# Window attention recurrence: the new score from an unnormalised sum, a maximum over the older scores, and each row held twice

## The chip, the cores and the metric

The kernel runs on one core of a Trainium2 chip. Its time is the device time of one execution, in microseconds (us). Three runs of the kernel before gave 2842.83, 2843.85 and 2847.93 us, a median of 2843.85 us. Engines: PE is TensorE, PEld its weight loads, DVE VectorE, ACT ScalarE, POOL GpSimd, SP the engine that issues most DMAs.

## The reference

The first layer is a recurrence over 1024 tokens in 4 sequences, with a window of 64. Only this layer is touched by the change. The rest of the program (a layer norm between, then a transformer layer with attention and a mixture of experts) takes the second half of the time.

```
q_local = feature @ wq_w + wq_b
def step(buf, q_i):                      # buf: the last 64 outputs
    ki = concat([buf, zeros((B, 1, D))], axis=1)          # 65 rows, the last is zero
    scores = einsum('bwd,d->bw', q_i[:, None, :] * ki, w2_w) + w2_b[0]
    alpha = softmax(scores, axis=1)
    v_i = einsum('bwd,bw->bd', ki, alpha)
    return concat([buf[:, 1:, :], v_i[:, None, :]], axis=1), v_i
_, vs = scan(step, feature[:, :64, :], q_local[:, 64:, :])
```

Each output is a weighted sum of the 64 outputs ahead of it, so token after token must be computed in turn: 960 steps.

## The kernel before

**Chunks and rows.** The 960 steps are 30 chunks (`NC`) of 32 rows (`L`). The kernel never forms an output inside the chunk's loop. It keeps, in `tab`, three tables of 96 columns: table 0 holds scores and tables 1 and 2 hold coefficients by which a row depends on the 64 outputs ahead of the chunk. The 128 partitions are 4 sequences of 32: for the scores, a partition is a future query of the chunk; for the coefficients, it is one of the older outputs. Since a row's output is linear in older outputs, its score against every later query is the same weighted sum of older scores. After a chunk, PE turns coefficients into outputs and computes the next chunk's first scores; that is work of a few us, mostly beside the loop.

**A step.** For row r of chunk c, with `k = r % 2`:

- ACT (L204) computes `ex = exp(row - max)` over 65 columns and its sum `z`. That is one instruction and a read of its accumulator.
- DVE then computes `rz = 1/z` (L292), the weighted sum of table 0 (helper `weighted`, L264, table 0), the *next* row's new score (L298: the sum of `ex * rz * row`, written straight into column 64 of `row`), the weighted sum of table 1 (L264), the next row's maximum (L306), the new score of table 0 times `rz` (helper `normalised`, L269, one column), the weighted sum of table 2 (L264), a shuffle that copies row r+2 of table 0 to all partitions of its sequence (L314), and the coefficients times `rz` (L269, two columns).

The order on DVE is written by hand; every engine takes its instructions in that order. `s_exp`, `s_rz`, `s_new`, `s_max`, `s_raw_score`, `s_score`, `s_row`, `s_raw` and `s_coef` are semaphores between them. Of two waits ahead of an operation, the first is an instruction of its own, and `sem_inc(s_pace, 1)` behind a `wait_ge` makes such a lone instruction too. `s_pace` itself is waited for by nobody.

**Row buffers.** `row` has two buffers of 66 columns: the next row's scores stand in columns 1 to 65, and columns 0 to 64 are the same scores as the row before it sees them, one place to the left.

Of the kernel before, what the change touches and what calls it, by code (L numbers as in the profile page):

```python
# [10 lines left out]
ALU = mybir.AluOpType  # L11
ACT = mybir.ActivationFunctionType
AX = mybir.AxisListType

P = 128
B, T, D = 4, 1024, 128
WIN = 64
L = 32
NK = T // L
NC = NK - WIN // L  # L20
ROW = WIN + 1
# [17 lines left out]
M_ROW = HD * PARTS  # L39
EPS = 1e-5  # L40


def window_attention(nc, io, xt, w, stacks, s_weights, moe_dram):

# [2 lines left out]
    with ctx:  # L47
        def sb(name, shape, dt=F32):
            return ctx.enter_context(nc.sbuf_tensor(name, shape, dt))
# [4 lines left out]
        def sem(name):  # L54
            return ctx.enter_context(nc.semaphore(name))
# [23 lines left out]


        tab = sb("tab", [P, 3, WIN + L])
        row = sb("row", [P, 2, ROW + 1])
        nmax = sb("nmax", [P, 2])
        ex = sb("ex", [P, 2, ROW])
        z = sb("z", [P, 2])
        rz = sb("rz", [P, 2])
        junk = sb("junk", [P, 4, ROW])
        raw = sb("raw", [P, 3])

        pf = ps("pf", [P, 2, 4 * P])  # L90
        pq = ps("pq", [P, 2, 4 * P])
# [11 lines left out]
        s_pace, s_pace_act = sem("s_pace"), sem("s_pace_act")  # L103
# [4 lines left out]
        s_scores = sem("s_scores")  # L108
        s_row, s_max, s_exp, s_rz, s_new, s_coef = (sem("s_row"), sem("s_max"), sem("s_exp"), sem("s_rz"),
                                                   sem("s_new"), sem("s_coef"))  # L110
        s_raw, s_raw_score, s_score = sem("s_raw"), sem("s_raw_score"), sem("s_score")
        s_clear = sem("s_clear")
        s_bdc, s_pv, s_vr, s_vall, s_pt, s_vt2, s_vt1, s_g, s_bdg = (
            sem("s_bdc"), sem("s_pv"), sem("s_vr"), sem("s_vall"), sem("s_pt"), sem("s_vt2"), sem("s_vt1"),
# [72 lines left out]
        @block.scalar  # L187
        def _(act):
            act.wait_ge(s_mv, NK)
            act.wait_ge(s_const, 2)  # L190
            nc.scalar.activation(std[:, :], mv[:, :, 1], ACT.Sqrt, bias=eps[:, :]).then_inc(s_std, 1)
            for g in range(8):
                act.wait_ge(s_ft, g + 1)
                if g >= 2:
                    act.wait_ge(s_pq, g - 1)
                if g == 2:
                    act.wait_ge(s_vt0, 2)
                nc.scalar.copy(ft[:, g % 2, :], pf[:, g % 2, :]).then_inc(s_ftc, 1)
            nc.scalar.preload_act_table(ACT.Exp)
            act.wait_ge(s_init, 14)  # L200
            for c in range(NC):
                for r in range(L):
                    act.wait_ge(s_max, L * c + r + 1)
                    nc.scalar.activation(ex[:, r % 2, :], row[:, r % 2, 1:], ACT.Exp, bias=nmax[:, r % 2:r % 2 + 1],  # L204
                                         accum_out=z[:, r % 2:r % 2 + 1]).then_inc(s_exp, 1)


                    if r == 1:
                        act.wait_ge(s_vall, c + 1)
                        act.sem_inc(s_pace_act, 1)  # L210
                        act.wait_ge(s_pv, c + 1)
                        nc.scalar.copy(vr[:, :], p_v[:, 0:D]).then_inc(s_vr, 1)
                    if r == 4:
                        act.wait_ge(s_vt2, c + 1)
                        act.sem_inc(s_pace_act, 1)
                        act.wait_ge(s_pt, c + 1)
                        nc.scalar.copy(vt1[:, :], p_t[:, 0:P]).then_inc(s_vt1, 1)
                    if 8 <= r < 8 + B:
                        act.wait_ge(s_g, c + 1)
                        q = slice(L * (r - 8), L * (r - 8) + L)  # L220
                        nc.scalar.copy(bdg[q, :, q], p_g[q, 0:2 * P].rearrange("p (g i) -> p g i", g=2)[:, :, q])\  # L221
                            .then_inc(s_bdg, 1)

        @block.vector
        def _(dve):
# [29 lines left out]
            for b in range(B):  # L255
                q = slice(L * b, L * b + L)
# [4 lines left out]

            def weighted(g, k, r, done):

                nc.vector.scalar_tensor_tensor(junk[:, g, :], ex[:, k, :], 1.0, tab[:, g, r:r + ROW], ALU.mult,  # L264
                                               ALU.mult, accum_out=raw[:, g:g + 1]).then_inc(done, 1)

            def normalised(g0, g1, k, r, done):

                nc.vector.tensor_tensor(tab[:, g0:g1, r + WIN:r + ROW], raw[:, g0:g1].unsqueeze(2),  # L269
                                        rz[:, k:k + 1].unsqueeze(1).broadcast_to((P, g1 - g0, 1)),  # L270
                                        ALU.mult).then_inc(done, 1)

            for c in range(NC):
                nc.vector.tensor_copy(tab[:, 0, WIN:], b0_row[:, :]).then_inc(s_table, 1)
                dve.wait_ge(s_scores, c + 1)
                nc.vector.tensor_scalar(tab[:, 0, 0:WIN], p_s[:, 0:WIN], b0[:, :], None, ALU.add).then_inc(s_table, 1)
                dve.wait_ge(s_table, 2 * (c + 1))
                dve.sem_inc(s_pace, 1)

                nc.vector.stream_shuffle(row[:, 0, 1:], tab[:, 0, 0:ROW], [0] * L).then_inc(s_row, 1)  # L280
                nc.vector.stream_shuffle(row[:, 1, :], tab[:, 0, 0:ROW + 1], [1] * L).then_inc(s_row, 1)
                dve.wait_ge(s_row, L * c + 1)
                nc.vector.reduce_max(nmax[:, 0:1], row[:, 0, 1:], AX.X, negate=True).then_inc(s_max, 1)

                dve.wait_ge(s_bdc, c + 1)
                nc.vector.memset(tab[:, 1:3, WIN:], 0.0).then_inc(s_clear, 1)
                dve.wait_ge(s_clear, c + 1)
                for r in range(L):
                    k, n = r % 2, L * c + r
                    last = r == L - 1  # L290
                    dve.wait_ge(s_exp, n + 1)
                    nc.vector.reciprocal(rz[:, k:k + 1], z[:, k:k + 1]).then_inc(s_rz, 1)  # L292
                    if not last:
                        weighted(0, k, r, s_raw_score)

                        dve.wait_ge(s_row, L * c + r + 2)
                        dve.wait_ge(s_rz, n + 1)
                        nc.vector.scalar_tensor_tensor(junk[:, 3, :], ex[:, k, :], rz[:, k:k + 1],  # L298
                                                       row[:, 1 - k, 0:ROW], ALU.mult, ALU.mult,
                                                       accum_out=row[:, 1 - k, WIN:ROW]).then_inc(s_new, 1)  # L300
                    if r:
                        dve.wait_ge(s_coef, n)
                    weighted(1, k, r, s_raw)
                    if not last:
                        dve.wait_ge(s_new, (L - 1) * c + r + 1)
                        nc.vector.reduce_max(nmax[:, 1 - k:2 - k], row[:, 1 - k, 1:], AX.X, negate=True)\  # L306
                            .then_inc(s_max, 1)
                        dve.wait_ge(s_raw_score, (L - 1) * c + r + 1)
                        normalised(0, 1, k, r, s_score)
                    weighted(2, k, r, s_raw)  # L310
                    if r < L - 2:
                        dve.wait_ge(s_score, (L - 1) * c + r + 1)
                        dve.sem_inc(s_pace, 1)
                        nc.vector.stream_shuffle(row[:, k, :], tab[:, 0, r + 1:r + 2 + ROW], [r + 2] * L)\  # L314
                            .then_inc(s_row, 1)
                    dve.wait_ge(s_raw, 2 * n + 2)
                    normalised(1, 3, k, r, s_coef)

            dve.wait_ge(s_pv, NC + 1)
            nc.vector.tensor_copy(v_all[:, NC + 2, :], p_v[:, 0:D]).then_inc(s_vr, 1)  # L320
# [1422 lines left out]
```

## Time and profile before

| | |
|---|---|
| median of 3 runs | 2843.85 us |
| profiled execution | 2847.15 us |
| span of its trace | 2845.3 us |
| DVE busy | 2248.1 us, 79% |
| ACT busy | 1286.1 us, 45% |
| PE busy | 1189.3 us, 42% |

The profiled execution is 3.3 us above the median. The busy time is the time covered by an engine's instructions. On DVE consecutive instructions overlap: the next begins before the one ahead of it has ended, so the distance from start to start is what an instruction takes of the engine, and the duration is what a waiting instruction has to wait for. Both are read from the timeline. A DVE or ACT instruction with an accumulator is two rows, the operation and the read of its accumulator; only at the end of the second is the sum there. Lone waits are not among the timeline's rows.

### The profile page before, as it was taken

To read this page: it belongs to the slowest core of one execution; us is meant where nothing else is said; L and a number is where in the kernel's file an instruction comes from. 1 tells how busy PE (TensorE), PEld (TensorE's weight loads), DVE (VectorE), ACT (ScalarE), POOL (GpSimd) and SP (SyncE) were. 2 spreads that over 40 slices of the span, in tenths; PEclk is the share of its full clock that TensorE was granted. 3 is DMA by queue.
4 is the path that set the end of the run, shared out by engine and by line. 5 is a ranking of instruction groups with operands and counts; after the bars stand their busy time and mean duration, and the time that the engine had idled before them with its cause. 6 is when DMAs were issued, how large, how long until landed. Compare 5 with 4: busy or idle time off the path is not lost. (4 is left out here: it accounts for less than half of the span.)

```text
span 2845.3 us, 38133 instructions
## 1 busy us (share of the span) xinstructions
PE 1189.3 (42%) x7272; PEld 529.5 (19%) x7272; DVE 2248.1 (79%) x15205; ACT 1286.1 (45%) x3230; POOL 287.0 (10%) x425
## 2 busy tenths in 40 slices
PE   3010100001010101000003787878877877787797
PEld 1000000000000000000001111223422333233365
DVE  5999999999999999999994789776767667765233
ACT  1333333333333333333361456557855676577742
POOL 0000000000000000000010020032113210321211
PEclk9999999999999999999997799889988898799998
DMA  5000000000000000000015012103110211100100
GB/s 136 1 1 1 1 1 1 1 1 1 1 1 1 1 1 1 1 1 1 1 32 133 8 31 56 20 21 82 38 44 21 65 46 30 33 23 27 41 1 23
DMA packets 80181, 66.13 MB, mean 23 GB/s; under 512 B 8702, under 2 KB 64808, under 8 KB 79944
## 3 DMA queue, kind: packets, MB, share of 16 engines
q1 hardware_dynamic: 76872, 57.40, 8.3%
q0 software_dynamic: 3072, 6.30, 0.7%
q14 instruction: 177, 1.45, 0.2%
q8 instruction: 60, 0.98, 0.1%
HBM read 34.77 MB, written 28.57 MB: 22 GB/s over the span
## 5 line engine op out<-in xcount | busy, mean ns | idle before, releaser
L1310 DVE TENSOR_REDUCE nm_half<-pair 128x2 f32<-128x1024 f32 x512 | 611.6, 1220 | 196.7 <-PE pair L1558 178.4
L204 ACT ACTIVATE ex<-row,nmax 128x65 f32<-128x65 f32 x960 | 336.1, 350 | 924.2 <-DVE nmax L306 837.6
L1198 ACT ACTIVATE pt<-pair 128x1024 f32<-128x1024 f32 x512 | 513.6, 1025 | 382.7 <-PE pair L1568 368.1
L264 DVE SCALAR_TENSOR_TENSOR junk<-ex,tab 128x65 f32<-128x65 f32 x2850 | 622.1, 219 | 1.4 <-issue 0.4
L367 PE MATMUL p_s<-tab,bdg 128*128 128x32 f32 x120 | 31.9, 406 | 829.4 <-DVE tab L269 829.4
L1534 PE MATMUL p_o<-pt,va 128*9 128x512 f32 x2048 | 298.4, 658 | 7.0 <-ACT pt L1198 7.0
L269 DVE TENSOR_TENSOR tab<-raw,rz 128x1 f32<-128x1 f32 (+1 forms) x1890 | 286.6, 152 | 3.2 <-issue 1.1
L298 DVE SCALAR_TENSOR_TENSOR junk<-ex,rz,row 128x65 f32<-128x65 f32 x930 | 265.5, 285 | 3.0 <-issue 2.7
L1558 PE MATMUL pair<-ks,qs 48*128 48x512 bf16 x1024 | 209.5, 420 | 111.7 <-ACT pt L1198 55.8
L264 DVE DVE_READ_ACCUMULATOR junk<-ex,tab 128x1 f32 x2850 | 236.8, 83 | 0.2
L1568 PE MATMUL pair<-qs,ks 50*128 50x512 bf16 x1024 | 210.8, 415 | 52.6 <-ACT pt L1198 22.1
L314 DVE STREAM_SHUFFLE row<-tab 128x66 f32<-128x66 f32 x900 | 207.0, 230 | 10.2 <-issue 2.6
L306 DVE TENSOR_REDUCE nmax<-row 128x1 f32<-128x65 f32 x930 | 200.6, 216 | 0.4
L367 PEld LDWEIGHTS p_s<-tab,bdg 128*128 128x128 f32 x120 | 27.9, 323 | 833.4 <-DVE tab L269 833.4
L204 ACT ACTIVATION_READ_ACCUMULATOR ex<-row,nmax 128x1 f32 x960 | 179.2, 187 | 0.0
L292 DVE RECIPROCAL rz<-z 128x1 f32<-128x1 f32 x960 | 157.1, 164 | 18.6 <-ACT ex L204 15.1
L182 POOL TENSOR_TENSOR bdc<-tab,mask 128x128 f32<-128x128 f32 x60 | 26.0, 455 | 1226.3 <-DVE tab L269 1226.3
L364 PE MATMUL p_s<-vt,qn 128*32 128x32 f32 x240 | 10.0, 251 | 255.2 <-ACT bdg L221 255.2
L1568 PEld LDWEIGHTS pair<-qs,ks 50*128 50x128 bf16 x1024 | 48.6, 95 | 304.9 <-DVE nm_half L1310 122.1
L1222 ACT ACTIVATE hid<-pair,bias_t 128x128 f32<-128x128 f32 x276 | 75.3, 383 | 28.6 <-PE pair L1633 28.4
L1558 PEld LDWEIGHTS pair<-ks,qs 48*128 48x128 bf16 x1024 | 49.5, 97 | 202.3 <-ACT pt L1198 91.8
L1633 PE MATMUL pair<-hid,yg 128*128 128x128 f32 x552 | 75.2, 292 | 25.5 <-DVE nm_half L1310 16.0
(254 smaller groups left out, 1951.1 us busy)
## 6 DMA issues: line engine op xcount, KB each, us to landing
parts_dram<-parts SPq DMA_DIRECT2D x48, 256.0 KB, 3.5
qs<-parts_dram SPq DMA_DIRECT2D x32, 192.0 KB, 4.7
ks<-parts_dram SPq DMA_DIRECT2D x32, 192.0 KB, 5.2
hid<-xs_dram SPq DMA_DIRECT2D x33, 128.0 KB, 2.1
ys_dram<-hid SPq DMA_DIRECT2D x33, 128.0 KB, 1.8
h_dram<-f SPq DMA_DIRECT2D x20, 128.0 KB, 2.5
x<-in_x SPq DMA_DIRECT2D x4, 512.0 KB, 8.3
w_W<-in_W SPq DMA_DIRECT2D x1, 2048.0 KB
```

Of the source, the lines that this page charges most:

```text
L204: nc.scalar.activation(ex[:, r % 2, :], row[:, r % 2, 1:], ACT.Exp, bias=nmax[:, r % 2:r % 2 + 1], accum_out=z[:, r % 2:r % 2 + 1]).then_i ...
L264: nc.vector.scalar_tensor_tensor(junk[:, g, :], ex[:, k, :], 1.0, tab[:, g, r:r + ROW], ALU.mult, ALU.mult, accum_out=raw[:, g:g + 1]).the ...
L269: nc.vector.tensor_tensor(tab[:, g0:g1, r + WIN:r + ROW], raw[:, g0:g1].unsqueeze(2), rz[:, k:k + 1].unsqueeze(1).broadcast_to((P, g1 - g0 ...
L292: nc.vector.reciprocal(rz[:, k:k + 1], z[:, k:k + 1]).then_inc(s_rz, 1)
L298: nc.vector.scalar_tensor_tensor(junk[:, 3, :], ex[:, k, :], rz[:, k:k + 1], row[:, 1 - k, 0:ROW], ALU.mult, ALU.mult, accum_out=row[:, 1 ...
L306: nc.vector.reduce_max(nmax[:, 1 - k:2 - k], row[:, 1 - k, 1:], AX.X, negate=True)\
L314: nc.vector.stream_shuffle(row[:, k, :], tab[:, 0, r + 1:r + 2 + ROW], [r + 2] * L)\
L1198: nc.scalar.activation(pt[:, kt % 2, :, tokens(t)], pair[fill.pair][:, :, :], ACT.Exp, scale=SCALE).then_inc(s_exp, 1)
L1310: nc.vector.reduce_max(nm_half[:, t, hp % 2, :, q], pair[fill.pair][:, :, :], AX.X, negate=True)\
L1534: ins = nc.tensor.matmul(p_o[j:j + VH, :], va[:, kt, 2 * (hp % HP) + par, :], pt[:, kt % 2, par, tokens(t)], start=kt == 0, stop=kt == QT - 1)
L1558: ins = nc.tensor.matmul(pair[fill.pair][:, par, :], qs[rows, hp % HP, tile(q)], ks[rows, hp % HP, tokens(t)], start=True, stop=True)
L1568: ins = nc.tensor.matmul(pair[fill.pair][:, par, :], ks[rows, hp, tile(kt)], qs[rows, hp, tokens(t)], start=True, stop=True)
```

## The change

It does the following, in the first layer alone:

- `weighted` holds the exponentials to `CAP` = 1e30 by a minimum instead of multiplying them by 1.
- The next row's new score is computed in two instructions: a weighted sum with unnormalised exponentials into `raw[:, 3]` (L313 of the new kernel), which stands ahead of the reciprocal, and a small operation on one column, `max(rz, 1/CAP) * raw` (helper `divided`, L274), which writes it into the row.
- `normalised` becomes `divided`, the same small operation as a `scalar_tensor_tensor`.
- The maximum (`largest`, L290) is over `row[:, :, 0, 1:]`, 64 columns without the new score, and stands ahead of the small operation that writes the new score. ACT waits for both the maximum and the new score.
- Each row buffer holds two copies, one as the row before sees it, the other shifted by one. One shuffle (`shifted`, L286) of 130 columns writes both, in place of one of 66.
- The order in a step is: sum for the new score, reciprocal, sum of table 0, maximum, new score, score into table 0, coefficients of the *row before*, shuffle, sums of tables 1 and 2.

```diff
+CAP = 1e30
...
-        row = sb("row", [P, 2, ROW + 1])
+        row = sb("row", [P, 2, 2, ROW])
...
-        raw = sb("raw", [P, 3])
+        raw = sb("raw", [P, 4])
...
                     act.wait_ge(s_max, L * c + r + 1)
-                    nc.scalar.activation(ex[:, r % 2, :], row[:, r % 2, 1:], ACT.Exp, bias=nmax[:, r % 2:r % 2 + 1],
+                    if r:
+                        act.sem_inc(s_pace_act, 1)
+                        act.wait_ge(s_new, (L - 1) * c + r)
+                    nc.scalar.activation(ex[:, r % 2, :], row[:, r % 2, 1, :], ACT.Exp, bias=nmax[:, r % 2:r % 2 + 1],
                                          accum_out=z[:, r % 2:r % 2 + 1]).then_inc(s_exp, 1)
...
-                nc.vector.scalar_tensor_tensor(junk[:, g, :], ex[:, k, :], 1.0, tab[:, g, r:r + ROW], ALU.mult,
+                nc.vector.scalar_tensor_tensor(junk[:, g, :], ex[:, k, :], CAP, tab[:, g, r:r + ROW], ALU.min,
                                                ALU.mult, accum_out=raw[:, g:g + 1]).then_inc(done, 1)
...
+            def divided(to, g0, g1, k, done):
+                nc.vector.scalar_tensor_tensor(to, rz[:, k:k + 1].unsqueeze(1).broadcast_to((P, g1 - g0, 1)),
+                                               1.0 / CAP, raw[:, g0:g1].unsqueeze(2), ALU.max, ALU.mult)\
+                    .then_inc(done, 1)
+            def coefficients(c, r):
+                dve.wait_ge(s_raw, 2 * (L * c + r) + 2)
+                divided(tab[:, 1:3, r + WIN:r + ROW], 1, 3, r % 2, s_coef)
+            def shifted(q, r):
+                src = tab[:, 0, r:r + ROW]
+                pair = bass.AP(src.tensor, src.offset, [src.ap[0], [1, 2], [1, ROW]])
+                nc.vector.stream_shuffle(row[:, q % 2, :, :], pair, [q] * L).then_inc(s_row, 1)
+            def largest(c, r):
+                dve.wait_ge(s_row, L * c + r + 1)
+                nc.vector.reduce_max(nmax[:, r % 2:r % 2 + 1], row[:, r % 2, 0, 1:], AX.X, negate=True)\
+                    .then_inc(s_max, 1)
...
                     dve.wait_ge(s_exp, n + 1)
+                    if not last:
+                        dve.wait_ge(s_row, n + 2)
+                        nc.vector.scalar_tensor_tensor(junk[:, 3, :], ex[:, k, :], CAP, row[:, 1 - k, 0, :], ALU.min,
+                                                       ALU.mult, accum_out=raw[:, 3:4]).then_inc(s_raw_new, 1)
                     nc.vector.reciprocal(rz[:, k:k + 1], z[:, k:k + 1]).then_inc(s_rz, 1)
                     if not last:
                         weighted(0, k, r, s_raw_score)
-
-                        dve.wait_ge(s_row, L * c + r + 2)
+                    if not last:
+                        largest(c, r + 1)
+                    if not last:
+                        dve.wait_ge(s_raw_new, m)
+                        dve.sem_inc(s_pace, 1)
                         dve.wait_ge(s_rz, n + 1)
-                        nc.vector.scalar_tensor_tensor(junk[:, 3, :], ex[:, k, :], rz[:, k:k + 1],
-                                                       row[:, 1 - k, 0:ROW], ALU.mult, ALU.mult,
-                                                       accum_out=row[:, 1 - k, WIN:ROW]).then_inc(s_new, 1)
+                        divided(row[:, 1 - k, 1, WIN - 1:WIN].unsqueeze(2), 3, 4, k, s_new)
+                    if not last:
+                        dve.wait_ge(s_raw_score, m)
+                        divided(tab[:, 0:1, r + WIN:r + ROW], 0, 1, k, s_score)
+                    if r:
+                        coefficients(c, r - 1)
+                    if r < L - 2:
+                        dve.wait_ge(s_score, m)
+                        dve.sem_inc(s_pace, 1)
+                        shifted(r + 2, r + 1)
                     if r:
                         dve.wait_ge(s_coef, n)
                     weighted(1, k, r, s_raw)
-                    if not last:
-                        dve.wait_ge(s_new, (L - 1) * c + r + 1)
-                        nc.vector.reduce_max(nmax[:, 1 - k:2 - k], row[:, 1 - k, 1:], AX.X, negate=True)\
-                            .then_inc(s_max, 1)
-                        dve.wait_ge(s_raw_score, (L - 1) * c + r + 1)
-                        normalised(0, 1, k, r, s_score)
                     weighted(2, k, r, s_raw)
-                    if r < L - 2:
-                        dve.wait_ge(s_score, (L - 1) * c + r + 1)
-                        dve.sem_inc(s_pace, 1)
-                        nc.vector.stream_shuffle(row[:, k, :], tab[:, 0, r + 1:r + 2 + ROW], [r + 2] * L)\
-                            .then_inc(s_row, 1)
-                    dve.wait_ge(s_raw, 2 * n + 2)
-                    normalised(1, 3, k, r, s_coef)
+                    if last:
+                        coefficients(c, r)
```

The order on DVE, one step inside a chunk of the kernel before, from its reciprocal to the next (L264 is `weighted` for tables 0, 1 and 2 in turn, L269 `normalised`):

```order
L292 RECIPROCAL rz<-z 128x1 [waits s_exp]
L264 SCALAR_TENSOR_TENSOR junk,raw<-ex,tab 128x65
L298 SCALAR_TENSOR_TENSOR junk,row<-ex,rz,row 128x65 [waits s_rz,s_row]
L264 SCALAR_TENSOR_TENSOR junk,raw<-ex,tab 128x65 [waits s_coef]
L306 TENSOR_REDUCE nmax<-row 128x1 [waits s_new]
L269 TENSOR_TENSOR tab<-raw,rz 128x1 [waits s_raw_score]
L264 SCALAR_TENSOR_TENSOR junk,raw<-ex,tab 128x65
L314 STREAM_SHUFFLE row<-tab 128x66 [waits s_score]
L269 TENSOR_TENSOR tab<-raw,rz 128x2 [waits s_raw]
L292 RECIPROCAL rz<-z 128x1 [waits s_exp]
```

The same stretch of the changed kernel, from the first instruction that waits for ACT to the next such (L269 is now `weighted`, L274 `divided`, L286 the shuffle, L290 the maximum):

```order
L313 SCALAR_TENSOR_TENSOR junk,raw<-ex,row 128x65 [waits s_row,s_exp]
L315 RECIPROCAL rz<-z 128x1
L269 SCALAR_TENSOR_TENSOR junk,raw<-ex,tab 128x65
L290 TENSOR_REDUCE nmax<-row 128x1 [waits s_row]
L274 SCALAR_TENSOR_TENSOR row<-rz,raw 128x1 [waits s_raw_new,s_rz]
L274 SCALAR_TENSOR_TENSOR tab<-rz,raw 128x1 [waits s_raw_score]
L274 SCALAR_TENSOR_TENSOR tab<-rz,raw 128x2 [waits s_raw]
L286 STREAM_SHUFFLE row<-tab 128x130 [waits s_score]
L269 SCALAR_TENSOR_TENSOR junk,raw<-ex,tab 128x65 [waits s_coef]
L269 SCALAR_TENSOR_TENSOR junk,raw<-ex,tab 128x65
L313 SCALAR_TENSOR_TENSOR junk,raw<-ex,row 128x65 [waits s_row,s_exp]
```

Nine instructions have become ten. The shuffle has moved ahead of the sums of tables 1 and 2, and between it and the score that it waits for (the one-column L274 that writes `tab`) there is now a two-column operation instead of a sum over 65 columns.

The last two rows of a chunk on DVE, in the changed kernel (from the sum of table 1 in row 30 to the copy that opens the next chunk's table):

```order
L269 SCALAR_TENSOR_TENSOR junk,raw<-ex,tab 128x65 [waits s_coef]
L269 SCALAR_TENSOR_TENSOR junk,raw<-ex,tab 128x65
L315 RECIPROCAL rz<-z 128x1 [waits s_exp]
L274 SCALAR_TENSOR_TENSOR tab<-rz,raw 128x2 [waits s_raw]
L269 SCALAR_TENSOR_TENSOR junk,raw<-ex,tab 128x65 [waits s_coef]
L269 SCALAR_TENSOR_TENSOR junk,raw<-ex,tab 128x65
L274 SCALAR_TENSOR_TENSOR tab<-rz,raw 128x2 [waits s_raw]
L294 COPY tab<-b_row 128x32
```

Here the coefficients of row 30 stand between the reciprocal of row 31 and its sums; before, they stood ahead of that reciprocal.

## Rows read from the trace of the kernel before

**Rows 1.** The page's busy times: engine, us, share of the span, instructions.

```profile
PE 1189.3 (42%) x7272; PEld 529.5 (19%) x7272; DVE 2248.1 (79%) x15205; ACT 1286.1 (45%) x3230; POOL 287.0 (10%) x425
```

**Rows 2.** Busy time by stretch, first layer's loop: stretch, length, each engine, clock, DMA.

```profile
56.90:1440.00 1383.10, 126.68 (x633) 95.61 (x634) 1297.33 (x13380) 457.43 (x2100) 49.09 (x150) 1.00 0.00 1
```

**Rows 3.** Waits of DVE, 58 to 1440 us: who, for whom: us, times, longest.

```profile
DVE rz L292 <- ACT ex L204: 15.1, 30, 0.6
DVE row L314 <- issue: 5.5, 15, 0.4
```

**Rows 4.** The same for ACT.

```profile
ACT ex L204 <- DVE nmax L306: 837.6, 930, 1.3
```

**Rows 5.** Timeline of one step: start us, duration us, engine, line, operation.

```profile
690.83 0.16 DVE L292 RECIPROCAL rz<-z 128x1 f32<-128x1 f32 x1
690.91 0.21 DVE L264 SCALAR_TENSOR_TENSOR junk<-ex,tab 128x65 f32<-128x65 f32 x1
691.04 0.08 DVE L264 DVE_READ_ACCUMULATOR junk<-ex,tab 128x1 f32 x1
691.11 0.28 DVE L298 SCALAR_TENSOR_TENSOR junk<-ex,rz,row 128x65 f32<-128x65 f32 x1
691.32 0.08 DVE L298 DVE_READ_ACCUMULATOR junk<-ex,rz,row 128x1 f32 x1
691.32 0.22 DVE L264 SCALAR_TENSOR_TENSOR junk<-ex,tab 128x65 f32<-128x65 f32 x1
691.46 0.09 DVE L264 DVE_READ_ACCUMULATOR junk<-ex,tab 128x1 f32 x1
691.46 0.22 DVE L306 TENSOR_REDUCE nmax<-row 128x1 f32<-128x65 f32 x1
691.60 0.15 DVE L269 TENSOR_TENSOR tab<-raw,rz 128x1 f32<-128x1 f32 x1
691.66 0.22 DVE L264 SCALAR_TENSOR_TENSOR junk<-ex,tab 128x65 f32<-128x65 f32 x1
691.71 0.35 ACT L204 ACTIVATE ex<-row,nmax 128x65 f32<-128x65 f32 x1 [0.92 <-DVE nmax L306]
691.80 0.09 DVE L264 DVE_READ_ACCUMULATOR junk<-ex,tab 128x1 f32 x1
691.90 0.01 DVE L314 LOAD_MASK_SELECT row<-tab  x1
691.92 0.23 DVE L314 STREAM_SHUFFLE row<-tab 128x66 f32<-128x66 f32 x1
691.97 0.19 ACT L204 ACTIVATION_READ_ACCUMULATOR ex<-row,nmax 128x1 f32 x1
692.06 0.15 DVE L269 TENSOR_TENSOR tab<-raw,rz 128x2 f32<-128x2 f32 x1
692.19 0.16 DVE L292 RECIPROCAL rz<-z 128x1 f32<-128x1 f32 x1
```

**Rows 6.** Timeline of DVE where a chunk begins.

```profile
702.41 0.28 DVE L276 TENSOR_SCALAR tab<-p_s,b 128x64 f32<-128x64 f32 x1 [1.07 <-PE p_s L367]
702.85 0.01 DVE L280 LOAD_MASK_SELECT row<-tab  x1 [0.15 <-DVE tab L276]
702.88 0.23 DVE L280 STREAM_SHUFFLE row<-tab 128x65 f32<-128x65 f32 x1
...
703.94 0.16 DVE L292 RECIPROCAL rz<-z 128x1 f32<-128x1 f32 x1 [0.50 <-ACT ex L204]
```

**Rows 7.** Timeline of DVE around row 30 of that chunk, and the next chunk.

```profile
745.17 0.15 DVE L269 TENSOR_TENSOR tab<-raw,rz 128x2 f32<-128x2 f32 x1
745.45 0.16 DVE L292 RECIPROCAL rz<-z 128x1 f32<-128x1 f32 x1
...
746.81 0.16 DVE L292 RECIPROCAL rz<-z 128x1 f32<-128x1 f32 x1
...
748.61 0.28 DVE L276 TENSOR_SCALAR tab<-p_s,b 128x64 f32<-128x64 f32 x1 [1.06 <-PE p_s L367]
```

More of the change, by code:

```diff
@@ L110, in window_attention @@
                                                    sem("s_new"), sem("s_coef"))
-        s_raw, s_raw_score, s_score = sem("s_raw"), sem("s_raw_score"), sem("s_score")
+        s_raw, s_raw_score, s_score, s_raw_new = sem("s_raw"), sem("s_raw_score"), sem("s_score"), sem("s_raw_new")
         s_clear = sem("s_clear")
@@ L262, in weighted @@
             def weighted(g, k, r, done):
-                nc.vector.scalar_tensor_tensor(junk[:, g, :], ex[:, k, :], 1.0, tab[:, g, r:r + ROW], ALU.mult,
+                nc.vector.scalar_tensor_tensor(junk[:, g, :], ex[:, k, :], CAP, tab[:, g, r:r + ROW], ALU.min,
                                                ALU.mult, accum_out=raw[:, g:g + 1]).then_inc(done, 1)
[L267 to L271, printed above, removed]
+            def divided(to, g0, g1, k, done):
[13 more added lines that the diff above has]
+                    .then_inc(s_max, 1)
             for c in range(NC):
@@ L278, in _ @@
                 dve.sem_inc(s_pace, 1)
-                nc.vector.stream_shuffle(row[:, 0, 1:], tab[:, 0, 0:ROW], [0] * L).then_inc(s_row, 1)
-                nc.vector.stream_shuffle(row[:, 1, :], tab[:, 0, 0:ROW + 1], [1] * L).then_inc(s_row, 1)
+                nc.vector.stream_shuffle(row[:, 0, 1, :], tab[:, 0, 0:ROW], [0] * L).then_inc(s_row, 1)
+                shifted(1, 0)
                 dve.wait_ge(s_row, L * c + 1)
-                nc.vector.reduce_max(nmax[:, 0:1], row[:, 0, 1:], AX.X, negate=True).then_inc(s_max, 1)
+                nc.vector.reduce_max(nmax[:, 0:1], row[:, 0, 1, :], AX.X, negate=True).then_inc(s_max, 1)
                 dve.wait_ge(s_bdc, c + 1)
@@ L288, in _ @@
                 for r in range(L):
-                    k, n = r % 2, L * c + r
+                    k, n, m = r % 2, L * c + r, (L - 1) * c + r + 1
                     last = r == L - 1
                     dve.wait_ge(s_exp, n + 1)
+                    if not last:
+                        dve.wait_ge(s_row, n + 2)
+                        nc.vector.scalar_tensor_tensor(junk[:, 3, :], ex[:, k, :], CAP, row[:, 1 - k, 0, :], ALU.min,
+                                                       ALU.mult, accum_out=raw[:, 3:4]).then_inc(s_raw_new, 1)
                     nc.vector.reciprocal(rz[:, k:k + 1], z[:, k:k + 1]).then_inc(s_rz, 1)
```

## The prediction

> **What bounds the kernel now.** I began with the page's busy times: DVE has 79% of the span, ACT 45% [rows 1]. Then the stretches: the first layer's loop takes 1383 of 2845 us, DVE is busy in 1297 of them, ACT in 457, and PE and POOL hardly at all [rows 2]. So everything that the change touches is one engine with hardly a gap, and one beside it that mostly waits. The waits say for what: ACT waits 837.6 us for the maximum of L306, once in each of 930 steps, while DVE waits for ACT only 30 times, once a chunk [rows 3, 4]. That looks like a loop bound by DVE alone, but the timeline of a step says something finer. From reciprocal to reciprocal a step takes 692.19 - 690.83 = 1.36 us. The reciprocal at 692.19 begins 0.03 after ACT's accumulator read has ended (691.97 + 0.19 = 692.16), and 0.13 after the two-column L269, though behind the one-column L269 the next instruction began after 0.06 [rows 5]. So ACT releases it, and DVE has about 0.06 us to spare in a step. Two things are nearly equal: the ring (reciprocal, L264, L298, L264, maximum, ACT, reciprocal), 1.36 us, and the time that DVE needs for its instructions, 1.30 us.
>
> **The ring after the change.** I put 0 at the start of the new sum L313 and go by starts in [rows 5], each good to 0.01. What an instruction takes of DVE: a sum with an immediate 0.145 (0.14 from 691.32 to 691.46, where the next begins together with the accumulator read; 0.15 can be the rounding), 0.13 for the one behind the reciprocal (690.91 to 691.04), the reciprocal 0.08, the maximum 0.135, a small operation 0.065. Reciprocal at 0.145, table 0 at 0.225, maximum at 0.355, new score at 0.49, done at 0.64 (0.15 long). ACT starts 0.03 behind its releaser (691.46 + 0.22 = 691.68, start 691.71), at 0.67; if the maximum (end 0.575) and the lone wait in front set it, hardly later. It needs 0.45 (691.71 to 692.16), so it has done at 1.12, and the next sum could start at about 1.16, or 1.22 with the lone wait of `s_exp` in front. So the change does what it says: the ring falls from 1.36 to 1.16 to 1.22. Gone from it are L298's longer stay (0.21 for 0.145, with the 0.07 ahead of it) and the sum of table 1.
>
> **What DVE needs.** New score at 0.49, score into table 0 at 0.555, ending at 0.705, coefficients at 0.62. Now comes the shuffle, which waits for that score, with a lone wait and then the mask load ahead of it. What this costs stands in the trace, since the same pair was there: L269 ended at 691.60 + 0.15 = 691.75, the mask load came at 691.90 and the shuffle at 691.92, 0.17 later; where a chunk begins and nothing else is in the way it is 702.69 to 702.88, 0.19 [rows 5, 6]. Before, the sum of table 2 (0.14) ran in that time; now only the two-column operation (0.065) does. So the shuffle starts at 0.705 + 0.175 = 0.88, and DVE issues nothing from 0.685 to 0.86. That stall of 0.17 is the heart of my forecast.
>
> The shuffle has 130 columns instead of 66. No row shows that size. Below, it takes of DVE what 66 columns do, 0.14 (691.92 to 692.06); above, two such, 0.28. Between them: 65 columns against 1 cost 0.145 against 0.065 for the two-tensor operations, 0.08 for 64 columns, so I take 0.14 + 0.07 = 0.21. Then come the two sums at 1.09 and 1.235, and the next L313 at 1.38. ACT has done at 1.12, long before.
>
> So the step is 1.38 us against 1.36: DVE now sets it. Ten roundings can put this off by about 0.02. The sums have 0.14 and 0.15 beside each other, and the place of the shuffle 0.17 and 0.19; leaning to the larger I take 1.385, 0.025 more than before. The ring's gain of 0.14 or more is lost behind DVE: saved there are 0.06 at L298 and 0.07 ahead of it, and paid are one instruction more (0.065), 0.07 of columns and about 0.08 of stall that a sum used to cover; against a step of 1.30 on DVE that is 0.08 more. `min` in place of `mult`, the maximum over 64 columns and `max` in the small operation change neither count nor columns: nothing. The third and further lone waits (in front of L313 for ACT, in front of the new score) are for events that came at least 0.1 us earlier, and I cost them at nothing because the sequencer meets them while the instruction ahead runs; if that cover is missing, each costs about what a lone wait adds between a satisfied release and its operation, 0.05 to 0.07 (L298 began 0.07 behind the accumulator read's start, where L306 began at once).
>
> **Chunk edges.** A chunk took 748.61 - 702.41 = 46.20 us [rows 6, 7]. The second shuffle at its start is longer by 0.07 and stands ahead of the first maximum: +0.07. Row 30 has no shuffle, so there the ring sets the end: about 1.16 instead of 1.38, -0.20 against before. In row 31 the coefficients of row 30 stand behind the reciprocal, and the sum of table 1 waits for them: 0.08 + 0.15 + 0.03 instead of 0.08, +0.18. Together +0.05 a chunk, 1.5 us in all. PE's and POOL's work between chunks is as before.
>
> **Fetch stalls.** 32 steps of 1.36 and the edges do not make up 46.20: now and then a step is longer, as at 745.45, where the reciprocal comes 0.28 behind L269 instead of 0.13 [rows 5, 7]; the profile names "issue" for 15 of those ahead of the shuffle alone [rows 3]. 46.20 - 1.53 (L276 at 702.41 to the first reciprocal) - 31 x 1.36 - 1.80 (the last reciprocal to L276 at 748.61) leaves 0.7 us a chunk, 21 us in all. With an instruction more in nine and nothing to spare, I estimate 3 to 6 more; I take 4.
>
> **Sum.** 900 steps with a shuffle x 0.025 = 22.5, edges 1.5, stalls 4: +28 us, within what a row rounded to 0.01 allows +30. On the profiled execution, 2847.15 + 30 = 2877; on the median, 3.3 lower, 2874 us.
>
> **Rivals.**
> - *The wait for the score is not paid; the ring sets the end (faster).* If DVE could issue mask and shuffle behind the coefficients without the 0.17, its need would be 1.38 - 0.17 = 1.21, and the ring 1.22 at most: -0.14 x 930 = -130 us, about 2714. For it: the ring does shorten, and the score's release falls in a part where DVE still has coefficients to do. Against: 0.17 and 0.19 in both places of the trace where this pair stands, once with nothing between. It decides from where the stall falls under 0.15 (no loss). Chance 0.09.
> - *Each instruction takes the least that a row shows, or the long shuffle no more than the short one.* With 0.13 for every sum and the maximum, 0.06 for a small operation and 0.20 for the shuffle the step is 1.315; with my prices and 0.14 for the shuffle it is the same. That is less than now: -0.045 x 900 + 5 = -35 us, 2809 on the median. For it: 0.13 does stand behind the reciprocal. Against: 0.14 and 0.15 stand behind the others [rows 5]. The Trainium skill (VectorE: DVE Perf Modes, the section on the TRN2 errata) has 58 cycles and one for each element, at 0.96 GHz, which is 0.128 for a sum, 0.061 for a small operation and 0.196 for this shuffle; by it the step would be 1.28 and the time about 2775. The rows are 0.01 to 0.02 above it for each sum, and with four of them, and a maximum, in a step that decides the sign. Chance 0.05.
> - *It comes out level:* the ten roundings fall the other way by 0.025 a step. 2838 to 2849. Chance 0.06.
> - *Lone waits are not covered, or the shuffle costs double.* +0.055 a step for the wait in front of L313 makes +50 on top of mine, about 2924; a shuffle of 0.28 makes +63, about 2937. For the first: behind table 0's sum the wait in front of L298 did cost 0.07. Against: that wait's own release, the reciprocal (end 690.99), came late enough to explain it. Chance 0.14.
> - *Each added DVE instruction costs a whole one.* Nine instructions take 1.36, 0.151 each; ten would take 1.51, +0.15 x 930 = +140, 2984. Against: instructions begin 0.14 apart though 0.22 long, and small ones 0.06 apart [rows 5]. The Trainium skill's rule that one should minimise the number of chained VectorE operations, since the pipe drains behind each (VectorE: DVE Perf Modes, "Rules for kernel authors"), speaks for it. Chance 0.03.
>
> My forecast has the remaining 0.63, with 2852 to 2900 as its own range. What a measurement of this kernel can tell from no change is about 0.2%, 6 us. Faster by more: 0.09 + 0.05 = 0.14. Within: 0.06. Slower, with 0.63, 0.14 and 0.03: 0.80. For 8 in 10 the range leaves out the faster cases and the highest: 2842 to 2922.
>
> **What would show it.** In the new timeline: L313 to L313 1.38 to 1.39 us; between the two-column L274 and the mask load DVE idle for about 0.17; shuffle to the next sum 0.21; ACT's accumulator read ending 0.2 or more ahead of the next L313, so that DVE waits for ACT in rows 31 and 0 alone; ACT's start set by the maximum or the new score near 0.67 to 0.73. It is wrong if the idle piece ahead of the mask load is missing, if L313 comes 0.03 to 0.1 behind ACT's end, or if L313 starts later than 0.15 behind the sum of table 2.

## The result, and the profile after

The changed kernel takes 2871.49 us (median of 4 runs, 2868.01 to 2876.24), the kernel before 2843.34 us (4 runs): a ratio of 1.0099, with a 95% interval of 1.0081 to 1.0117. That is 28 us slower, and the interval leaves out no change. The forecast was 2874 us, 30 more than the kernel before.

The page of the changed kernel, its busy times, answers to [rows 1]:

```profile
PE 1179.6 (41%) x7272; PEld 526.0 (18%) x7272; DVE 2208.3 (77%) x16135; ACT 1286.0 (45%) x3230; POOL 288.9 (10%) x425
```

DVE has 930 instructions more, one a step, and is busy 40 us *less*. That does not tell what was added: busy time is what the instructions cover with their full length, not what they take of the engine. Where DVE really stands can be read only from start to start, in a step. The timeline of the changed kernel (start us, duration us, engine, line, operation), from the new sum L313 ahead of one reciprocal to the next reciprocal, answers to [rows 5]; L274 x2 is the table's score and the coefficients:

```profile
699.22 0.22 DVE L313 SCALAR_TENSOR_TENSOR junk<-ex,row 128x65 f32<-128x65 f32 x1
699.36 0.08 DVE L313 DVE_READ_ACCUMULATOR junk<-ex,row 128x1 f32 x1
699.36 0.16 DVE L315 RECIPROCAL rz<-z 128x1 f32<-128x1 f32 x1
699.44 0.21 DVE L269 SCALAR_TENSOR_TENSOR junk<-ex,tab 128x65 f32<-128x65 f32 x1
699.57 0.08 DVE L269 DVE_READ_ACCUMULATOR junk<-ex,tab 128x1 f32 x1
699.57 0.22 DVE L290 TENSOR_REDUCE nmax<-row 128x1 f32<-128x64 f32 x1
699.70 0.15 DVE L274 SCALAR_TENSOR_TENSOR row<-rz,raw 128x1 f32<-128x1 f32 x1
699.77 0.23 DVE L274 SCALAR_TENSOR_TENSOR tab<-rz,raw 128x1 f32<-128x1 f32 x2
699.91 0.35 ACT L209 ACTIVATE ex<-row,nmax 128x65 f32<-128x65 f32 x1 [0.94 <-DVE row L274]
700.08 0.01 DVE L286 LOAD_MASK_SELECT row<-tab  x1
700.10 0.30 DVE L286 STREAM_SHUFFLE row<-tab 128x130 f32<-128x130 f32 x1
700.16 0.19 ACT L209 ACTIVATION_READ_ACCUMULATOR ex<-row,nmax 128x1 f32 x1
700.30 0.22 DVE L269 SCALAR_TENSOR_TENSOR junk<-ex,tab 128x65 f32<-128x65 f32 x1
700.45 0.08 DVE L269 DVE_READ_ACCUMULATOR junk<-ex,tab 128x1 f32 x1
700.45 0.22 DVE L269 SCALAR_TENSOR_TENSOR junk<-ex,tab 128x65 f32<-128x65 f32 x1
700.60 0.09 DVE L269 DVE_READ_ACCUMULATOR junk<-ex,tab 128x1 f32 x1
700.60 0.22 DVE L313 SCALAR_TENSOR_TENSOR junk<-ex,row 128x65 f32<-128x65 f32 x1
700.74 0.08 DVE L313 DVE_READ_ACCUMULATOR junk<-ex,row 128x1 f32 x1
700.74 0.16 DVE L315 RECIPROCAL rz<-z 128x1 f32<-128x1 f32 x1
```

The step is 1.38 us. ACT has done at 700.35, and the sum that needs it starts at 700.60, 0.25 later, behind DVE's own work: DVE sets the step. The table's score starts at 699.77 and ends at about 699.92; the shuffle starts at 700.10, and ahead of the mask load nothing is issued for about 0.17. The timeline draws half of that stretch as filled, since the two small operations together last until 700.00. Only the distance from start to start shows all of it.

Counted in this way, DVE stood in three places of a step before: 0.10 ahead of the mask load (the sum of table 2 at 691.66 takes 0.14, the mask load comes at 691.90), 0.07 ahead of L298 and 0.06 ahead of the reciprocal, 0.22 in all. Now it stands in one place, for 0.17. So DVE waits a little less than before, and its instructions take about 0.07 more of it: a small operation (0.065) and 64 columns (0.07) were added, and L298's longer stay (0.065) is gone. The new stall ahead of the shuffle uses up what the shorter waits elsewhere gave.

The same timeline at the end of a chunk and the start of the next, which answers to [rows 6, 7]:

```profile
704.87 0.16 DVE L315 RECIPROCAL rz<-z 128x1 f32<-128x1 f32 x1
...
705.89 0.16 DVE L315 RECIPROCAL rz<-z 128x1 f32<-128x1 f32 x1
705.97 0.15 DVE L274 SCALAR_TENSOR_TENSOR tab<-rz,raw 128x2 f32<-128x2 f32 x1
706.15 0.23 DVE L269 SCALAR_TENSOR_TENSOR junk<-ex,tab 128x65 f32<-128x65 f32 x1
...
707.88 0.28 DVE L296 TENSOR_SCALAR tab<-p_s,b 128x64 f32<-128x64 f32 x1 [1.07 <-PE p_s L389]
...
708.49 0.29 DVE L286 STREAM_SHUFFLE row<-tab 128x130 f32<-128x130 f32 x1
708.69 0.21 DVE L303 TENSOR_REDUCE nmax<-row 128x1 f32<-128x65 f32 x1
...
709.62 0.16 DVE L315 RECIPROCAL rz<-z 128x1 f32<-128x1 f32 x1
```

Row 30, without a shuffle, takes 1.02 us, and the last reciprocal to the next L296 1.99 in place of 1.80.

From the starts of all 960 reciprocals in the two traces, with the median of each row of a chunk as its regular length (us, first to last reciprocal):

| part | before | after | difference |
|---|---|---|---|
| rows 0 to 29 (1.360 to 1.376 in most) | 1226.0 | 1241.7 | +15.8 |
| row 30 (1.359 to 1.019) | 40.8 | 30.6 | -10.2 |
| between chunks (3.32 to 3.74) | 96.4 | 108.4 | +12.0 |
| all above the medians | 16.0 | 24.0 | +8.0 |
| sum | 1379.2 | 1404.7 | +25.6 |

The last part is the steps that are now and then 0.1 to 0.4 us longer. In the trace before, 72 of the 74 that are over 0.09 us lie a multiple of 128 recorded DVE instructions apart, lone waits and accumulator reads included. That they are pauses to fetch instructions fits, but no run tests it. The page's queue for instructions (packets, MB, share) grew by an eighth. Before:

```profile
q14 instruction: 177, 1.45, 0.2%
```

After:

```profile
q14 instruction: 199, 1.63, 0.2%
```

### The profile page after: what moved, and what is told of

Its sections match the earlier page's. It is cut to its first block and busy times, and to the rows that moved or that the text cites. A ratio compares the mean times of both kernels' runs of the same rounds, so it can differ in the third digit from the quotient of the medians.

```text
span 2868.4 us, 40893 instructions
## 1 busy us (share of the span) xinstructions
PE 1179.6 (41%) x7272; PEld 526.0 (18%) x7272; DVE 2208.3 (77%) x16135; ACT 1286.0 (45%) x3230; POOL 288.9 (10%) x425
## 5 line engine op out<-in xcount | busy, mean ns | idle before, releaser
L269 DVE SCALAR_TENSOR_TENSOR junk<-ex,tab 128x65 f32<-128x65 f32 x2850 | 545.7, 217 | 4.7
L286 DVE STREAM_SHUFFLE row<-tab 128x130 f32<-128x130 f32 x930 | 279.9, 301 | 8.2 <-issue 0.2
L269 DVE DVE_READ_ACCUMULATOR junk<-ex,tab 128x1 f32 x2850 | 236.4, 83 | 0.0
L274 DVE SCALAR_TENSOR_TENSOR tab<-rz,raw 128x1 f32<-128x1 f32 (+1 forms) x1890 | 221.4, 156 | 2.5
L313 DVE SCALAR_TENSOR_TENSOR junk<-ex,row 128x65 f32<-128x65 f32 x930 | 206.7, 222 | 15.6 <-DVE tab L305 15.3
L290 DVE TENSOR_REDUCE nmax<-row 128x1 f32<-128x64 f32 x930 | 200.6, 216 | 0.1
L274 DVE SCALAR_TENSOR_TENSOR row<-rz,raw 128x1 f32<-128x1 f32 x930 | 140.0, 151 | 2.4 <-issue 2.4
```

What stands on the lines that cost most here:

```text
L269: nc.vector.scalar_tensor_tensor(junk[:, g, :], ex[:, k, :], CAP, tab[:, g, r:r + ROW], ALU.min, ALU.mult, accum_out=raw[:, g:g + 1]).then ...
L274: nc.vector.scalar_tensor_tensor(to, rz[:, k:k + 1].unsqueeze(1).broadcast_to((P, g1 - g0, 1)), 1.0 / CAP, raw[:, g0:g1].unsqueeze(2), ALU ...
L286: nc.vector.stream_shuffle(row[:, q % 2, :, :], pair, [q] * L).then_inc(s_row, 1)
L290: nc.vector.reduce_max(nmax[:, r % 2:r % 2 + 1], row[:, r % 2, 0, 1:], AX.X, negate=True)\
L313: nc.vector.scalar_tensor_tensor(junk[:, 3, :], ex[:, k, :], CAP, row[:, 1 - k, 0, :], ALU.min, ALU.mult, accum_out=raw[:, 3:4]).then_inc( ...
```

## The experiments

My theory: DVE sets the step; the time from the end of the table's score to the shuffle, 0.177 us, is paid because only one small operation stands in it; and 64 more columns in the shuffle are paid as well. The rivals: the count of instructions decides, or the ring through ACT still does. Steps below are medians of rows 2 to 28. For comparison, the kernel before ran beside these on the same chips, at 2840.79 us (7 runs) beside "The score of table 0 first", "A lone wait less", "One copy of each row" and "A sum in the gap", and at 2842.81 us (15 runs) beside the other four.

**The score of table 0 first.** Two small operations change places, on top of the kernel called "A lone wait less" below, which the text of this expectation calls "the one before":

```diff
                     if not last:
-                        dve.wait_ge(s_raw_new, m)
-                        divided(row[:, 1 - k, 1, WIN - 1:WIN].unsqueeze(2), 3, 4, k, s_new)
-                    if not last:
                         dve.wait_ge(s_raw_score, m)
                         divided(tab[:, 0:1, r + WIN:r + ROW], 0, 1, k, s_score)
+                    if not last:
+                        dve.wait_ge(s_raw_new, m)
+                        divided(row[:, 1 - k, 1, WIN - 1:WIN].unsqueeze(2), 3, 4, k, s_new)
```

> As the one before, and the score of table 0 stands ahead of the new score of the next row, not behind it: the same instructions, two of them exchanged. Theory (the stall ahead of the shuffle counts from the end of the table's score): the score ends 0.065 earlier, so does the shuffle; step 1.31, time about 2812 us (2803 to 2822). Rival (count of instructions): step 1.375, 2871 us. Rival (ring through ACT): the next row's new score is 0.065 later, step 1.44, 2930 us.

Measured: 2798.26 us (2790.59 to 2803.84), ratio to before 0.9848 (0.9818 to 0.9879); step 1.305. The same operations, 0.07 us less a step. That the count or the ring sets the step is excluded: by the count it would have stayed, by the ring it would have risen. From this kernel's timeline:

```profile
741.68 0.15 DVE L274 SCALAR_TENSOR_TENSOR tab<-rz,raw 128x1 f32<-128x1 f32 x1
741.74 0.15 DVE L274 SCALAR_TENSOR_TENSOR row<-rz,raw 128x1 f32<-128x1 f32 x1
741.81 0.15 DVE L274 SCALAR_TENSOR_TENSOR tab<-rz,raw 128x2 f32<-128x2 f32 x1
741.98 0.01 DVE L286 LOAD_MASK_SELECT row<-tab  x1
742.00 0.30 DVE L286 STREAM_SHUFFLE row<-tab 128x130 f32<-128x130 f32 x1
```

The score ends at 741.83, and the mask load follows 0.15 and the shuffle 0.17 behind it, as in both other kernels; now two small operations run in that time.

**A lone wait less.** This changes the waits alone; the kernel above must be read against it:

```diff
             def largest(c, r):
-                dve.wait_ge(s_row, L * c + r + 1)
...
+                        dve.wait_ge(s_rz, n + 1)
                         largest(c, r + 1)
...
                         dve.wait_ge(s_raw_new, m)
-                        dve.sem_inc(s_pace, 1)
-                        dve.wait_ge(s_rz, n + 1)
                         divided(row[:, 1 - k, 1, WIN - 1:WIN].unsqueeze(2), 3, 4, k, s_new)
```

> The changed kernel without the lone wait and increment in front of the new score: the maximum waits for the reciprocal instead (its wait for the row was double), and the new score waits for its sum alone. Theory (a lone wait whose event has come runs while the instruction ahead runs, and costs nothing): step stays 1.375 us within 0.005, time 2871 within 8 us. Rival (each lone wait costs 0.05 to 0.07): step 1.31 to 1.325, time 2811 to 2825 us.

Measured, one run: 2860.02 us; step 1.375, unchanged, as expected. The time is 11 us below the changed kernel, outside the 8 that I had given. In its trace what lies above the medians inside the chunks is 17.0 us in place of 23.4, and the instruction queue has 192 packets in place of 199. So a lone wait whose event has come costs a regular step nothing. That it adds to the longer steps is likely but not shown: in the four traces with 17081 recorded DVE instructions in the loop these came to 19.9 to 26.6 us, in the three with one lone wait a step less to 17.0 to 18.3 us. That is one trace for each kernel, and the first four scatter by as much as is to be explained. The shorter time also takes a share of the credit from the exchange above: against 2860 us the exchange alone is worth 62 us, and the theory said 59.

**The coefficients moved out of the gap.** The line for the coefficients stands directly behind the reciprocal:

```diff
                     nc.vector.reciprocal(rz[:, k:k + 1], z[:, k:k + 1]).then_inc(s_rz, 1)
+                    if r:
+                        coefficients(c, r - 1)
...
-                    if r:
-                        coefficients(c, r - 1)
```

> The changed kernel with the coefficients of the row before directly behind the reciprocal, in place of between the table's score and the shuffle: the same instructions, one of them moved. Theory (the stall ahead of the shuffle counts from the end of the table's score, and the coefficients ran inside it for nothing): the score comes 0.066 later, the step 1.44, the time about 2929 us (2918 to 2940). Rival (count of instructions): 1.375, 2871 us.

Measured, one run: 2939.94 us, step 1.447, 0.072 more for the same instructions. Inside the gap that operation was free; outside it costs its place, and so the number of instructions that DVE must take outside a stall does count.

**One copy of each row.** The undoing of one part of the change (the lines that only follow the buffer's new shape are left out, here and in the next two kernels that change it):

```diff
-        row = sb("row", [P, 2, 2, ROW])
+        row = sb("row", [P, 2, ROW + 1])
...
-                nc.vector.stream_shuffle(row[:, q % 2, :, :], pair, [q] * L).then_inc(s_row, 1)
+                nc.vector.stream_shuffle(row[:, q % 2, :], tab[:, 0, r:r + ROW + 1], [q] * L).then_inc(s_row, 1)
...
-                nc.vector.reduce_max(nmax[:, r % 2:r % 2 + 1], row[:, r % 2, 0, 1:], AX.X, negate=True)\
+                nc.vector.reduce_max(nmax[:, r % 2:r % 2 + 1], row[:, r % 2, 1:WIN], AX.X, negate=True)\
```

> The changed kernel with one copy of each row (66 columns as before the change, in place of 130); the maximum is over the 63 older scores ahead of the own column, so that the new score can be written beside it. Theory (the shuffle takes one element a cycle, and its 64 columns more are paid in full on DVE): step 1.375 - 0.067 = 1.308 us, 2 us less at the chunk starts too, time about 2809 us (2800 to 2818). Rival (they are hidden behind something else that sets the step): 1.375, 2871 us.

Measured: 2804.35 us (2802.16 to 2808.17), ratio 0.9874 (0.9851 to 0.9898); step 1.308. The 64 columns cost 0.068 us a step. That is 61 us in 900 steps; the loops of the two profiles differ by 60 us, the medians by 67 us. Without these columns the change would have been a gain of 36 us.

**The doubled row in the kernel before.** The same cost, put where the ring sets the step:

```diff
-                        nc.vector.stream_shuffle(row[:, k, :], tab[:, 0, r + 1:r + 2 + ROW], [r + 2] * L)\
+                        nc.vector.stream_shuffle(row[:, k, :, :], tab[:, 0, r + 1:r + 2 + ROW].unsqueeze(1)
+                                                 .broadcast_to((P, 2, ROW + 1)), [r + 2] * L)\
```

> The kernel before, with its shuffle of 66 columns writing two copies (132 columns), of which the second is read by nobody: the doubled row alone. Theory (the kernel before is bound by the ring through ACT, with 0.06 us to spare on DVE): 0.069 more on DVE takes the spare time and makes the step 1.36 to 1.37, time 2841 to 2852 us. Rival (DVE sets the step before as well): step 1.43, 2903 us.

Measured: 2846.77 us against 2842.81, ratio 1.0009 (0.9996 to 1.0022); step 1.363. 66 more columns, 0.003 us a step: the kernel before had the 0.06 us to spare on DVE. From its timeline, where the two-column L269 is now followed by the reciprocal after 0.07, as a small operation is when nothing holds up the next one, in place of the 0.13 of [rows 5]:

```profile
741.29 0.30 DVE L314 STREAM_SHUFFLE row<-tab 128x132 f32<-128x132 f32 x1
741.50 0.15 DVE L269 TENSOR_TENSOR tab<-raw,rz 128x2 f32<-128x2 f32 x1
741.57 0.15 DVE L292 RECIPROCAL rz<-z 128x1 f32<-128x1 f32 x1
```

**A sum in the gap: a miss.** In the changed kernel, the coefficients of the row before go ahead of the maximum, and the sum of table 1 between the table's score and the shuffle:

```diff
                         weighted(0, k, r, s_raw_score)
+                    if r:
+                        coefficients(c, r - 1)
...
-                    if r:
-                        coefficients(c, r - 1)
+                    if r:
+                        dve.wait_ge(s_coef, n)
+                    weighted(1, k, r, s_raw)
                     if r < L - 2:
                         dve.wait_ge(s_score, m)
                         dve.sem_inc(s_pace, 1)
                         shifted(r + 2, r + 1)
-                    if r:
-                        dve.wait_ge(s_coef, n)
-                    weighted(1, k, r, s_raw)
```

> Same instructions as the changed kernel, in another order: the coefficients of the row before stand ahead of the maximum, and the sum of table 1 stands between the new score of table 0 and the shuffle. Theory (DVE sets the step, and the 0.17 us from the end of the table's score to the shuffle is paid because nothing fills it): the sum of table 1 fills 0.145 of it, the score itself comes 0.065 later, so the step falls from 1.375 to about 1.30 and the time from 2871 to about 2803 us (2790 to 2815), under the kernel before. Rival (each DVE instruction costs its share, whatever the order): step 1.375, 2871 us. Rival (the ring through ACT sets the step): the new score comes 0.065 later, so 2930 us.

Measured: 2861.11 us (2860.51 to 2868.15), ratio 1.0077 (1.0051 to 1.0103); step 1.370. None of the three numbers I had written down, and by the time alone the count rival looked right. The timeline says otherwise:

```profile
701.14 0.01 DVE L286 LOAD_MASK_SELECT row<-tab  x1
701.16 0.30 DVE L286 STREAM_SHUFFLE row<-tab 128x130 f32<-128x130 f32 x1
701.37 0.22 DVE L269 SCALAR_TENSOR_TENSOR junk<-ex,tab 128x65 f32<-128x65 f32 x1
701.51 0.08 DVE L269 DVE_READ_ACCUMULATOR junk<-ex,tab 128x1 f32 x1
701.58 0.23 DVE L313 SCALAR_TENSOR_TENSOR junk<-ex,row 128x65 f32<-128x65 f32 x1
```

The sum of table 1 is in the gap, but L313 now starts 0.07 behind the accumulator read, where it began together with it in the changed kernel. It reads the row that the shuffle writes: 701.16 + 0.30 = 701.46, and 0.11 to 0.12 until it runs, a lone wait among it. I had reckoned with what the shuffle takes of DVE (0.205) and not with how long its result takes to land (0.30, and the lone wait). With two sums between, that was covered; with one it is not. A new wait had taken the old one's place.

**The reciprocal ahead of that sum.** One exchange in the kernel that missed, to test this reading. With it the reciprocal takes the wait for ACT and the sum the wait for the row, so the lone wait ahead of that sum is gone as well:

```diff
+                    nc.vector.reciprocal(rz[:, k:k + 1], z[:, k:k + 1]).then_inc(s_rz, 1)
                     if not last:
                         dve.wait_ge(s_row, n + 2)
                         nc.vector.scalar_tensor_tensor(junk[:, 3, :], ex[:, k, :], CAP, row[:, 1 - k, 0, :], ALU.min,
                                                        ALU.mult, accum_out=raw[:, 3:4]).then_inc(s_raw_new, 1)
-                    nc.vector.reciprocal(rz[:, k:k + 1], z[:, k:k + 1]).then_inc(s_rz, 1)
```

> The kernel in which the sum of table 1 fills the gap ahead of the shuffle (2861 us, step 1.370), with the reciprocal ahead of the new sum instead of behind it. Theory: there the new sum waited for the 130-column shuffle to land (0.30 long, and 0.11 from its end to the sum), with only one sum between; the reciprocal now stands in that time, the sum comes 0.08 later, and the step falls to 1.29 to 1.30, the time to about 2795 us (2785 to 2805). Rival (the landing is not what held it): step 1.370, 2861 us.

Measured, one run: 2797.72 us, step 1.300. What held the other was the wait for the row. Whether the reciprocal in between or the missing lone wait ended it, this kernel does not tell; from the shuffle's start the shuffle, one sum and the reciprocal take 0.42 of DVE in its trace, which would have covered 0.30 + 0.11 too, but only just.

**All of it.** What is kept of the change, the unnormalised sum and the maximum over older scores, with one copy of the row and an order in which every wait has work ahead of it (of the diff, the added lines; those that were moved stood elsewhere before):

```diff
                     dve.wait_ge(s_exp, n + 1)
                     nc.vector.reciprocal(rz[:, k:k + 1], z[:, k:k + 1]).then_inc(s_rz, 1)
                     if not last:
                         weighted(0, k, r, s_raw_score)
                     if not last:
+                        dve.wait_ge(s_row, n + 2)
+                        nc.vector.scalar_tensor_tensor(junk[:, 3, :], ex[:, k, :], CAP, row[:, 1 - k, 0:ROW], ALU.min,
+                                                       ALU.mult, accum_out=raw[:, 3:4]).then_inc(s_raw_new, 1)
...
                     weighted(1, k, r, s_raw)
                     weighted(2, k, r, s_raw)
+                    if r < L - 2:
+                        dve.wait_ge(s_score, m)
+                        dve.sem_inc(s_pace, 1)
+                        shifted(r + 2, r + 1)
+                    coefficients(c, r)
```

> Unnormalised sum and maximum over older scores kept, one copy of each row (66 columns), and a new order: reciprocal, sum of table 0, sum for the new score, maximum, new score, table's score, sums of tables 1 and 2, shuffle, this row's coefficients; one lone wait in place of three. Theory: the two sums (0.29) fill the 0.17 between score and shuffle, the landing of the row is covered by two instructions of the next row, and DVE needs about 1.14 us; the ring through ACT then is 0.35 (maximum starts) + 0.22 + 0.03 + 0.09 + 0.44 + 0.03 = 1.16 and sets the step. Time 2841 - 0.20 x 29.5 rows x 30 = about 2664 us (2650 to 2690). Rival (each instruction costs its share, ten instructions): 1.31 as with one copy, 2804 us. Rival (a wait that is not seen yet takes its place, as the row's landing did when only the gap ahead of the shuffle was filled): 1.25 or more, 2745 us or more.

Measured: 2663.33 us (5 runs, 2657.95 to 2669.30), ratio to before 0.9371 (0.9355 to 0.9388): 180 us less than before, 208 less than the changed kernel, which did not run beside it; step 1.167. Its timeline, both engines:

```profile
700.46 0.16 DVE L308 RECIPROCAL rz<-z 128x1 f32<-128x1 f32 x1 [0.51 <-ACT ex L209]
...
700.82 0.21 DVE L287 TENSOR_REDUCE nmax<-row 128x1 f32<-128x63 f32 x1
700.95 0.15 DVE L274 SCALAR_TENSOR_TENSOR row<-rz,raw 128x1 f32<-128x1 f32 x1
701.01 0.15 DVE L274 SCALAR_TENSOR_TENSOR tab<-rz,raw 128x1 f32<-128x1 f32 x1
...
701.15 0.35 ACT L209 ACTIVATE ex<-row,nmax 128x65 f32<-128x65 f32 x1 [0.80 <-DVE row L274]
...
701.38 0.01 DVE L284 LOAD_MASK_SELECT row<-tab  x1
701.38 0.23 DVE L284 STREAM_SHUFFLE row<-tab 128x66 f32<-128x66 f32 x1
701.40 0.18 ACT L209 ACTIVATION_READ_ACCUMULATOR ex<-row,nmax 128x1 f32 x1
701.51 0.15 DVE L274 SCALAR_TENSOR_TENSOR tab<-rz,raw 128x2 f32<-128x2 f32 x1
701.62 0.16 DVE L308 RECIPROCAL rz<-z 128x1 f32<-128x1 f32 x1
```

The shuffle starts directly behind the sums, its mask load with it. ACT starts 0.69 behind the reciprocal instead of 0.88, ends at 701.58, and the reciprocal follows 0.04 later: the ring sets the step again, with 0.11 from L274 to the reciprocal in place of the 0.07 that a small operation takes, so DVE has about 0.04 to spare.

## Why the prediction was right, step by step

- *ACT releases the reciprocal before, and DVE has 0.06 to spare.* Right, and shown: 66 columns more in the kernel before cost 0.003 us a step.
- *The ring falls to 1.16 to 1.22.* Right in the trace after: ACT starts 699.91 - 699.22 = 0.69 behind the L313 at 699.22 (0.67 to 0.73 was forecast) and ends 1.13 behind it. With DVE out of its way a ring of this kind ran at 1.167.
- *The stall ahead of the shuffle, 0.17.* Right, and the step that decided: with the score 0.07 earlier the step lost 0.07, with it 0.07 later it gained 0.07.
- *The long shuffle takes 0.21.* Right: 0.205 from start to start, 0.068 of them for the columns. With the short one the same kernel is faster than before, 2804 us.
- *Satisfied lone waits cost nothing.* Right for the regular step. For the stalls it is open.
- *The step grows by 0.025.* It grew by 0.016: the bare sum, 1.38, was right, and leaning to the larger reading was not. 900 steps make +15.8 in place of +22.5. (The second row of a chunk, beside which POOL's copies run, is longer than the rest in both traces and grew by 0.05.)
- *Chunk edges +1.5.* Measured -10.2 + 12.0 = +1.8. Row 30 fell by 0.34, not by 0.20, because its reciprocal now stands behind L313 and so starts 0.147 later in row 30 and not in row 31; the same 0.147 comes back at the next chunk's start.
- *Stalls +4, 3 to 6.* Measured +8.0, so the forecast was too low. I counted one instruction more in nine; the trace has two more a step, 18 recorded in place of 16, a small operation and a lone wait. By that count alone the 16 us would grow by 2, not by 8. That DVE has nothing to spare in which a pause could hide is a reason that fits; no run tests it.

Part of the closeness is luck. Two terms were off by 7 and 4 us in opposite directions. The terms were worked out for the profiled execution, where their sum of 28 (taken as 30) stands against 25.6 in the loop and 23.0 in the whole program (2870.18 against 2847.15 us); only the medians differ by 28.

The rival that I gave most for the faster side, that the wait for the score is not paid, is excluded by the two kernels that move the score. The one with the least price for each instruction, step 1.315, fails by the step of 1.376 and by its rows: three of the sums took 0.14 to 0.15 and the shuffle 0.20 to 0.21. The one that lone waits or a double shuffle add 50 us or more is excluded as well. The instruction count alone is no measure of this loop: the same ten operations a step ran at 1.447, 1.375, 1.300 and, with the narrow shuffle, 1.308 and 1.167 us. The Trainium skill's rule to minimise the number of chained VectorE operations and not the semaphores (VectorE: DVE Perf Modes, "Rules for kernel authors") is not enough here: at equal count, the order around the waits was worth up to 0.147 us a step.

## What to carry to other kernels

A chain made shorter gives its time only if the engine it runs on has that time to spare; add up distances from start to start on that engine, the waits within them included, before counting the gain. For every wait, list what stands between the release and the waiter: here 0.17 us from the end of a small operation to the shuffle that reads it, and 0.30 + 0.11 for the shuffle's own landing. Moving work into one of these uncovers the other unless both are counted. And a helper copy that removes a conflict (a row kept twice) is paid in columns on the bound engine; letting the maximum read one column less removed the same conflict for nothing.

## What the runs showed that was not expected

- TensorE's granted clock in the first layer's loop was 1.00 (2.4 GHz) in the profile of before [rows 2] and 0.50 (1.2 GHz) in that of the changed kernel (the same view, its last three columns clock, DMA share and GB/s), whose mean over the run was 0.69. The higher clock gained nothing: the changed kernel's runs at a mean of 0.69 took 2870.18 and 2868.01 us, those at 0.95 took 2876.24 and 2872.80. Between chunks DVE waited 1.07 us for PE's matmuls at either level ([rows 6], and L296 above).

```profile
50.70:1460.00 1409.30, 126.22 (x634) 95.34 (x634) 1257.55 (x14310) 457.56 (x2100) 50.94 (x150) 0.50 0.00 1
```

- A lone wait that is free in the step may still have a price. Taking 930 of them away left the step at 1.375 us and brought the loop from 1404.7 to 1397.4 us, in one profile each. Which part of this is the lone wait is not settled, as said above.
